# A gated relational graph layer on one core: smaller scans, two scales for the first weight, ScalarE in the closing of u, and a short path for tiles that only fill a turn

## The reference

```python
h = maximum(layernorm(x), 0)
u = h @ root + bias
for r in range(8):
    mask = edge_type == r
    sums = segment_sum(h[src] * mask[:, None], dst)     # [1250, 1024]
    cnt = segment_sum(mask, dst)
    u += (sums / maximum(cnt, 1)[:, None]) @ weight[r]
z = concatenate([u, h]) @ w_gate + b_gate
out = x + tanh(u) * z + h * (1 - z)
```

## Time and profile before

| | |
|---|---|
| median of 3 runs | 1389.53 us (1387.79 to 1394.82) |
| the profiled execution | 1388.87 us |
| its span, first to last instruction | 1387.1 us |
| granted TensorE clock, mean | 0.98 |
| busy: TensorE, VectorE, ScalarE, GpSimd | 1286.5, 962.9, 405.1, 791.4 us |
| moved by DMA | 269.42 MB, 194 GB/s |

### The profile page before, as it was taken

The page is one execution under the profiler, slowest core; times in us unless marked ns, Lnnn a source line. Parts: engine busy times, 40 slices in busy tenths (PEclk is TensorE's granted clock), DMA queues, the critical chain, the costliest instruction groups (busy, mean ns, idle before and its releaser), DMA issues.

```text
span 1387.1 us, 20131 instructions
## 1 busy us (share of the span) xinstructions
PE 1286.5 (93%) x6205; PEld 649.5 (47%) x6205; DVE 962.9 (69%) x1253; ACT 405.1 (29%) x496; POOL 791.4 (57%) x880
## 2 busy tenths in 40 slices
PE   2988889999999999999999999999899889988898
PEld 1434334444444445555554545444445444434565
DVE  5888678456564765677557767566575647998886
ACT  5344113224333430432232233222311211454100
POOL 2424078786878685777768766866675544431000
PEclk9999999999999999999999999999999999999999
DMA  6443115215214458776767888588786996677976
GB/s 224 155 172 107 44 38 173 63 45 174 54 45 116 131 171 272 238 224 193 246 211 231 270 276 284 162 296 272 230 259 218 349 304 182 207 250 220 250 228 188
DMA packets 112473, 269.42 MB, mean 194 GB/s; under 512 B 22678, under 2 KB 23181, under 8 KB 112388
## 3 DMA queue, kind: packets, MB, share of 16 engines
q1 hardware_dynamic: 75204, 175.63, 37.8%
q0 software_dynamic: 37184, 92.64, 23.6%
HBM read 203.66 MB, written 87.30 MB: 210 GB/s over the span
## 4 chain that ended last, share of the span: by engine, by line
PE 58%; DVE 14%; DMA 11%; issue 8%; POOL 4%; ACT 3%; POOLq 1%; DVEq 0%; SPq 0%; ACTq 0%
PE ps L1343 49%; DMA early<-y_rows,pair 9%; PE ps L1305 8%; DVE W L972 2%; POOL early L638 1%; DVE hT L1025 1%; POOL onehot L646 1%; DVE hT L1020 1%; POOL pair L628 1%; ACT W L752 1%; DMA early<-u_rows 1%; DVE yhl L1094 1%; ACT peek_out L719 1%; DVE urow L1185 1%; ACT early L762 1%
## 5 line engine op out<-in xcount | busy, mean ns | idle before, releaser
L1343 PE MATMUL ps<-W,hT 128*128 128x512 f16 (+2 forms) x4740 | 1073.5, 384 | 13.0 <-DVE W L972 13.0
L1343 PEld LDWEIGHTS ps<-W,hT 128*128 128x128 f16 (+2 forms) x4740 | 477.2, 103 | 532.9 <-issue 37.5
L638 POOL DMA_INDIRECT early<-y_rows,pair x200 | 240.4, 1202 | 132.1 <-PE ps L1308 81.6
L611 POOL DMA_INDIRECT table_rows<-edges,table_i x160 | 239.2, 1495 | 99.8 <-issue 99.8
L1305 PE MATMUL ps<-early,onehot 128*125 x800 | 206.8, 386 | 29.3 <-POOL onehot L646 15.5
L646 POOL TENSOR_SCALAR onehot<-iota_d,pair 128x125 f16<-128x125 f16 x188 | 160.8, 855 | 69.1 <-DMA early<-y_rows,pair 62.6
L972 DVE SCALAR_TENSOR_TENSOR W<-W,wsc 128x2048 f16<-128x2048 f32 x62 | 146.4, 2363 | 18.0 <-ACT W L752 18.0
L1305 PEld LDWEIGHTS ps<-early,onehot 128*125 x800 | 107.0, 137 | 103.9 <-issue 52.9
L752 ACT ACTIVATE W<-W,wsc 128x2048 f16<-128x2048 f32 x62 | 122.7, 1991 | 103.9 <-DVE W L988 51.3
L802 ACT ACTIVATE yhl<-early 128x512 f16<-128x512 f32 x100 | 62.8, 628 | 305.5 <-DVE early L1094 182.8
L719 ACT ACTIVATE peek_out<-W 128x1024 bf16<-128x1024 f32 x80 | 84.3, 1053 | 128.7 <-DMA W<-in_L_gnn_weight_dram 61.9
(11 more groups left out here) (187 smaller groups left out, 839.4 us busy)
## 6 DMA issues: line engine op xcount, KB each, us to landing
y_rows<-yhl SPq DMA_DIRECT2D x144, 256.0 KB, 2.7
W<-in_L_gnn_weight_dram SPq DMA_DIRECT2D x30, 1024.0 KB, 7.9
u_rows<-early SPq DMA_DIRECT2D x50, 448.0 KB
early<-u_rows SPq DMA_DIRECT2D x30, 448.0 KB
W<-in_L_gnn_w_gate_dram SPq DMA_DIRECT2D x8, 1024.0 KB, 7.1
early<-in_x_dram SPq DMA_DIRECT2D x9, 512.0 KB, 4.5
hs_rows<-early SPq DMA_DIRECT2D x9, 512.0 KB, 3.2
root_rows<-yhl SPq DMA_DIRECT2D x18, 256.0 KB, 5.5
```

What stands on the lines that cost most here:

```text
L611: pool.indirect_dma_start(out=table_rows, out_offset=bass.IndirectOffsetOnAxis(ap=at_i[:, c:c + 1], axis=0), in_=packed[0:EP, c:c + 1], in ...
L638: pool.indirect_dma_start(out=G[:, b, :], out_offset=None, in_=y_rows[i], in_offset=bass.IndirectOffsetOnAxis(ap=idx[:, b, :], axis=0), bo ...
L1343: last = nc.tensor.matmul(ps[0:rows, n % 4, :], hT[:, m, v_h, k, n0:n0 + rows], Wh[MAT[w][c]][:, v_w, k, :], start=(first and v_h + v_w == ...
```

## The change

- **Half scales.** Weight 0 gets one scale for its left half (quadrants 0, 1) and one for its right half (quadrants 2, 3). The lists ahead of unit 0 are written anew: one x tile and two quadrants first; `LEAD` goes from 2 to 3, with tile 1's transposes in the middle of unit 0, and the second scale's matmul behind unit 0. The first four units become (0,0), (1,0), (0,1), (1,1) in (row tile, half). SP issues x0, quadrants 0 and 1, x1, quadrants 2 and 3. `add_group` of relation 0 uses two reciprocals and two multiplies of 512 columns.
- **Small scans.** `scan_part` takes 16 parts of 5 groups (800 elements), spread over units 6 to 17; the keys come at unit 3; totals and bounds at units 18 and 20 (14 and 16 before). GpSimd fills the scan's factors behind row tiles 0 and 1. `positions` comes at units 22, 25, 28 and 32, after the low halves of weights in VectorE's list.
- **The sweeps** start at unit 113, not 100, and end where they did; the first three are packed closer.
- **Closing of u.** ScalarE sums the absolute values of the row (`u_size`) in place of VectorE's maximum, and ScalarE copies both banks out.
- **Fill tiles.** A sweep is rounded up so that at least one tile of its last turn is spare; TensorE's loop for the last group stops at the last tile with edges (`t_end`), and the spare tiles get only the count's matmul (`empty_tile`). GpSimd gathers and builds one-hots for them as before.

```diff
-    AGG_AT = ([100 + g * 63 // 30 for g in range(30)] + [164 + g * 42 // 20 for g in range(20)]
-              + [208 + g * 40 // 20 for g in range(20)] + [249 + g * 20 // 10 for g in range(10)])
+    AGG_AT = ([113 + g * 57 // 30 for g in range(30)] + [170 + g * 38 // 20 for g in range(20)]
+              + [209 + g * 39 // 20 for g in range(20)] + [249 + g * 21 // 10 for g in range(10)])
...
-    LEAD = 2
-    NORM_AT = {0: 2, 1: 3, 3: 4, 5: 5, 7: 6, 8: 7, 10: 8, 12: 9}
-    TURN_AT = {1: 2, 3: 3, 5: 4, 7: 5, 9: 6, 10: 7, 12: 8, 14: 9}
+    LEAD = 3
+    NORM_AT = {1: 3, 3: 4, 5: 5, 7: 6, 8: 7, 10: 8, 12: 9}
+    TURN_AT = {2: 2, 4: 3, 5: 4, 7: 5, 9: 6, 10: 7, 12: 8, 14: 9}
...
-    KEYS_AT, SCAN_AT, TOTALS_AT, BOUNDS_AT = 2, {4: 0, 7: 1, 10: 2, 12: 3}, 14, 16
-    POSITIONS_AT = {18: 0, 22: 1, 26: 2, 30: 3}
+    SN = 16
+    KEYS_AT, TOTALS_AT, BOUNDS_AT = 3, 18, 20
+    SCAN_AT = {6: (0, 1), 8: (2,), 9: (3,), 11: (4, 5), 12: (6,), 13: (7, 8), 14: (9,), 15: (10, 11), 16: (12, 13), 17: (14, 15)}
+    POSITIONS_AT = {22: 0, 25: 1, 28: 2, 32: 3}
...
             load_x(0)
+            for q in range(2):
+                land(0, q)
             load_x(1)
-            for q in range(4):
+            for q in range(2, 4):
                 land(0, q)
...
+            store_h(2)
+            load_x(4)
...
+            def u_size(j):
+                act.wait_ge(s["u_rooted"], j + 1)
+                if j:
+                    act.wait_ge(s["u_summed"], j)
+                nc.scalar.activation(u_abs[0:DT, :], cu[j % NCU][0:DT, :], ACT.Abs,
+                                     accum_out=urow[0:DT, j % 2:j % 2 + 1]).then_inc(s["u_summed"], 1)
...
-                act.wait_ge(s["uT_a"], j + 1)
                 act.wait_ge(s["gemm_done"], phase_end(W_GH, 1 if j < HT else 3))
-                nc.scalar.activation(hT[:, m, :, :, n0:n0 + DT],
...
+                for bank, turned, out_of in ((4, "uT_a", "uT_a_out"), (5, "uT_b", "uT_b_out")):
+                    act.wait_ge(s[turned], j + 1)
+                    nc.scalar.activation(hT[:, m + bank - 4, :, :, n0:n0 + DT],
...
-            for i in range(LEAD):
-                norm(i)
-            for i in range(LEAD):
-                turn_out(i)
+            norm(0)
             peek(0, 0)
-            peek(0, 1)
-            for c in range(4):
-                high_weights(0, c)
+            turn_out(0)
+            high_weights(0, 0)
+            high_weights(0, 1)
+            norm(1)
+            peek(0, 2)
+            turn_out(1)
+            high_weights(0, 2)
+            high_weights(0, 3)
+            norm(2)
...
-                step(nc.vector.tensor_scalar(turn_f[:, 0, 0:NS], ps[:, 7, NG:NG + NS], (RING - 1) / 2, 1.0 / RING, ALU.add, ALU.mult))
+                step(nc.vector.tensor_scalar(turn_f[:, 0, 0:NS], ps[:, 7, NG:NG + NS], (RING + 1) / 2, 1.0 / RING, ALU.add, ALU.mult))
...
             def row_scale(j):
-                u = cu[j % NCU][0:DT, :]
-                dve.wait_ge(s["u_rooted"], j + 1)
-                step(nc.vector.tensor_reduce(urow[0:DT, 0:1], u, AX.X, ALU.max, apply_absolute_value=True))
+                dve.wait_ge(s["u_summed"], j + 1)
...
+            stats_of(0)
+            first_peek(1)
+            dve.wait_ge(s["consts"], NCONST)
+            weight_top(0, 0)
+            weight_scale(0, 0)
+            turn_out(0)
+            stats_of(1)
+            low_weights(0, 0)
+            low_weights(0, 1)
             first_peek(3)
-            dve.wait_ge(s["consts"], NCONST)
-            weight_top(0)
-            weight_scale(0)
-            for c in range(4):
-                low_weights(0, c)
+            weight_top(0, 1)
+            turn_out(1)
+            weight_scale(0, 1)
+            stats_of(2)
+            low_weights(0, 2)
+            low_weights(0, 3)
...
+            def empty_tile(t):
+                pe.wait_ge(s["tile_ready"], t + 1 + RING)
+                hot_t = onehot[:, :, :].rearrange("p b n -> p (b n)")[:, bass.ds((t % RING) * P, DT)]
+                nc.tensor.matmul(ps[0:DT, 6, 0:2], hot_t, ones_h[:, :], start=False, stop=True,
+                                 skip_group_check=True).then_inc(s["onehot_free"], 1)
...
+                t_end = pe.value_load(bounds[0:1, NG + 1 + sweep:NG + 2 + sweep], min_val=2, max_val=TMAX)
+                with pe.Fori(t0 + 1, t_end) as t:
                     sum_tile(t, False)
+                with pe.Fori(t_end, t1) as t:
+                    empty_tile(t)
```

117 lines of the change are left out of this document (63 added, 54 removed).

## The result

The kernel after takes 1382.4 us (median of 10 executions, 1375.9 to 1383.8); the kernel before, with the executions added beside it, 1389.7 (10 executions, 1385.4 to 1394.8). The ratio is 0.9937, 95% interval 0.9917 to 0.9957: 6 to 12 us faster, where 41 were forecast. The forecast of 1348 and its range to 1370 both miss. Two of its own three alarms went off: the sweeps took over 630 us, and the closing still took 118 us or more.

The account below looks back on a forecast made before the run. The prediction took TensorE's product loop, busy 93% of the span, as the bound. Start 28, less 5 for new stops, plus 6.6 spare tiles and 12 closing gave 41.6 us off 1388.9: 1347.3, stated as 1348, range 1330 to 1370.

Parts of the forecast that it names:

- three alarms: Forecast wrong if unit 20 starts after 160, sweeps exceed 630 us, or closing's u transposes take 118 us or more.
- The start: Up to unit 20: first product at 22.2, unit 20 at 148.8 against 177.1, so 28 us sooner (16 to 33).
- 3.1 + 4 + 8: Losses charged before unit 20: 3.1 us stop before unit 2, 4 us slow matmuls, 8 us lost to VectorE.
- The aggregation's start: Positions at 160.5, GpSimd's scatters not moved; TensorE at unit 113 at 502.7, GpSimd at about 497, so 28 us stand.
- (c): Rival, units 4 to 19: VectorE bounds as before, 20 us lost, not 8; sums start 12 us later: 1360, chance 0.12.
- (d): Rival, slower: table late, each us of unit 22's finishes after 160.5 is lost; at 49 us late 1396, chance 0.03.
- (e): Rival, start: stays at 29.8 because quadrant 1 lands no sooner: 1355, chance 0.08.
- The sweeps: 13 units come out of the first three sweeps; 5 us of new stops charged (0 to 15).
- (a): Rival, sweeps: GpSimd's pace bounds them, they end where they did and only the closing gains: 1377, chance 0.10.
- Spare tiles: Sweep ends: 12 tiles that only fill up get the count's matmul alone, gaining 6.6 us (3 to 8.6).
- The closing: Closing of u: moving work from VectorE to ScalarE gains 12 us (3 to 19).
- (b): Rival, closing: gives 3 us, because VectorE then waits for ScalarE's size: 1357, chance 0.12.

Follow-up runs that it names:

- the repeated kernel: The kernel after, unedited, run again on another chip: 1379.1 us, ratio to before 0.9924.
- light feed: Every gather fetches only one row and one-hots are built in two columns: on the kernel after 1356.5 us, on the kernel before 1362.7 us.
- e1: The kernel after with the aggregation's groups back at the units of the kernel before, first at unit 100: 1386.5 us, ratio to before 0.9981.
- wide ends: The kernel after with four or five product units between sweeps, not two or three: 1376.9 us; with one-row gathers and two-column one-hots too, 1351.3 us.
- another lag: The kernel after with a tile's one-hot built after two more gathers instead of three, 1477.0 us, or after four, 1410.6 us.

## Why the prediction was wrong, point by point

**The start, right as a sum.** Forecast: unit 20 at 148.8; it starts at 149.7, 27.4 us sooner. Inside, two errors cancel. The first product is 4.2 us late on the forecast, and the rows show where. All engines in order of time, in the kernel after,

```profile
11.64 2.75 POOL L604 MEMSET hT<- 125x3180 bf16 x1
...
12.99 4.38 DVE L980 TENSOR_SCALAR wspread<-ones_f,wtop 128x128 f32<-128x128 f32 x1
...
14.38 2.79 POOL L604 MEMSET hT<- 125x3180 bf16 x1
17.10 0.19 POOL L605 MEMSET hT<- 125x20 bf16 x1
```

and in the kernel before:

```profile
22.71 0.28 DVE L950 TENSOR_SCALAR wspread<-ones_f,wtop 128x128 f32<-128x128 f32 x1
```

The peeks are done at 12.7 us, near the forecast's 12.4. Then the small step that spreads the maximum takes 4.38 us and not 0.28, and ends 0.08 us after GpSimd's fill of the scan's factors, which the change moved there from behind row tiles 2 and later. The same pair meets again at 31 us (5.09 us, to the end of the next fill), and in all eighteen profiles here with the new start the step takes 4.2 to 4.6 us, in the two with the old start 0.28 or 0.29. The prediction had put this move at nothing, as GpSimd "waits for tiles anyway"; it did not ask what VectorE does beside it. No run moves the fills alone, so the cause is read from these rows and not tested. From the scale to the first product it then takes 6.8 us, where 7.0 were forecast. The later losses are smaller: 123.3 us from first product to unit 20, less 111.5 of work, is 11.8, where 3.1 + 4 + 8 were charged. The granted clock is 1.00 there, 0.92 before.

**The aggregation's start, right.** The first scatter is at 176.3 (forecast 175.7), the first count at 504.1 (forecast 503.6). Rivals (c) and (d) fall with these two points, and (e) with the first product at 26.4. A small term hid a cancellation: the groups of VectorE that answer to the earlier trace rows, in the kernel after,

```profile
L1057 DVE TENSOR_TENSOR_SCAN hT<-hT 125x800 bf16<-125x800 bf16 x16 | 29.2, 1824 | 0.6
L1052 DVE TENSOR_TENSOR hT<-edges,iota_g 125x800 fp8e4<-125x800 f32 x16 | 17.6, 1103 | 0.0
```

take 46.8 us together, the four and four of before 46.7, so that the 24 more instructions seem to cost 0.1 us, where 4.8 were charged. But the mean of 8.18 us of a scan before is a mix:

```profile
L1025 DVE TENSOR_TENSOR_SCAN hT<-hT x4: 6824/8630/8632, 69.0 to 130.8; 125x3200 bf16<-125x3200 bf16 x4
```

(shortest, median and longest in ns). The 6.82 us scan has no work of GpSimd beside it; each of the three of 8.63 has GpSimd's low part of a row tile (L586) beside its start. Undisturbed, four small scans take 7.30 us for 6.82, and four small compares 3.92 (0.98 each in the middle of the sixteen) for 3.48: 0.15 to 0.16 us more for each added instruction, 3.7 us for 24. An estimate by the fixed latency of every instruction with an SBUF source (the Trainium skill, VectorE: DVE Perf Modes, The TRN2 errata — SBUF-src ops pay a fixed extra latency per instruction) is 3.8 us, and the trace agrees. What made it good again are the three stretched scans of before, 5.4 us, less 2.0 us of two compares that are stretched after (1.67 and 2.27 us).

**The sweeps, the step that failed.** "It is close. I charge 5 us of new stops (0 to 15)" was the term; it measured 17 to 24 us. The sweeps should have fallen by the 33.7 us of 13 units; they fell by 10.1 in this pair of profiles, so 24 came back as stops, and by 17.1 with the repeated kernel, so 17. (By the loss it is 32 and 25, 69.5 or 62.5 less 37.4, because the 8.6 us of the spare tiles are counted in it; they stand below as a term of their own.) The step compared means, 2.04 us for a tile on GpSimd against 2.8 to 3.1 that a tile would get, and took the idle 16.4 us of the second sweep as a reserve that can be spent. It isn't one. GpSimd waits because the ring is full, and TensorE waits at other times because it is empty (83.0 and 29.1 us in the same sweeps of the kernel after): tiles come in bursts of two or three, a new sweep needs three gathers before its first one-hot, and each gather needs some 6 us to land. The nearest rival, (a), had the place right and the reason too narrow: it held GpSimd's pace fixed, but with the light feed GpSimd waits 188 us for TensorE, and 31 us of extra loss are still there (up to 8.6 of them the spare tiles'). The gathers did not stretch more than before: they average 1191 ns, 1202 before, and 15 of 200 take over 1.5 us in either kernel. These 15 all have a long pass of VectorE beside them, while those with no VectorE instruction over 0.4 us beside them take 1.11 at most. That fits the port lock between VectorE and GpSimd (the Trainium skill, Trainium Architecture — The Big Picture, What this means for kernel authors), as the stretched steps of VectorE above do; that it would stretch gathers more as VectorE's work is packed closer is not borne out.

What is shown: 13 units fewer in the sweeps bring 15 to 22 us of loss at the same code (e1 beside the kernel after and its repeat), and neither light feed, nor wide ends, nor another lag returns it. What is only argued: that the rest at light feed, some 15 us inside the sweeps, is TensorE's own setting up of a group and its wait for VectorE's add, uncovered because the tiles come just in time. The waits named "issue" (5.7 us, 0.7 in the kernel before with the light feed, 11.6 with wide ends) and on L1215 (6.8, beside 4.5) point there; nothing here tests it. A rival is left for this part: with the light feed the new tile code itself may cost more than the 1 us of e1. The kernel with the old places and the light feed, which would tell, was not run.

**Spare tiles, mis-sized.** 6.6 us forecast, none measured. The prediction had named the reason (the last one-hots cost GpSimd 0.8 us each) and took only 2 of 8.6 us off for it. The rows at 729 to 731 us show it: the short matmuls come 0.7 us apart, at GpSimd's pace, and what TensorE saves it waits for at the next sweep's first one-hot.

**The closing, mis-sized.** 12 us forecast, 3.0 in the stage, none in the time. This is rival (b), at its price. VectorE did fall, from 109.3 to 94.3 us busy, and the 6.07 us stop on its copy is gone. Who VectorE waited for in that stage:

```profile
DVE uexp L1220 <- ACT edges L822: 11.4, 5, 3.3
DVE early L1228 <- ACT early L830: 6.4, 5, 3.2
DVE hT L1177 <- DMA hT<-zh_rows: 4.6, 1, 4.6
```

and TensorE:

```profile
PE ps L1378 <- ACT hT L844: 5.1, 3, 2.7
PE ps L1385 <- DVE hT L1188: 3.5, 2, 2.0
PE ps L1313 <- DVE wspread L980: 3.4, 1, 3.4
```

VectorE was spared 15 us of work, and waits 11.4 for ScalarE's size of u (L822), which it did not wait for before; on ScalarE's high part (L830) it waits 6.4, 3.7 before. The prediction took half of the stage's loss as the gain by VectorE's share, where the work was a chain from engine to engine, and moving a link of it does not shorten it.

In all: the 28 held; the 5 should have been 24 in this pair, the 6.6 nothing and the 12 should have been 3. 28 - 24 + 0 + 3 = 7 us, which is what was measured. That the 28 held is in part luck, as 4.1 us lost in the spreading step were made good by smaller losses behind it. Rivals (a) and (b) both held in their effect; together the prediction had them at 1386 and gave that 0.03, when they should have been weighed as likely: both ask only that waiting time on an engine is no slack.

## What to carry to other kernels

Independent matmuls that lie between dependent ones are cover, and pulling them out to another place saves only as much as the chain they covered does not need: before counting a stage shorter, add up what each piece of the feed takes at its worst (here three gathers and their landing at a sweep's start: 7.8 us from the last spare tile at 730.7 to the first tile at 738.5), not at its mean. An engine that waits in a full ring has no slack if its reader waits on the empty ring in the same stage. When a step is moved to a time in which its own engine is free, look at what the other engines do just then. And test a theory of a shared cost on the kernel before as well: the light feed on the new kernel alone seemed to prove one that the same feed on the old one refuted.

## What was not expected of the hardware

The lag is much sharper than its 6 us of landing suggests: one gather less ahead costs 95 us, 0.47 a tile, one more costs 28.

Short stops are dearer than they look, as the matmuls behind a stop run slower: after the 4.64 us stop the four matmuls of a tile take 1.96 us, and 1.03 to 1.07 elsewhere. It is the clock. The kernel after by stretch: the last products before the stop, the stop, the first tiles behind it, and two stretches more (columns as in the earlier trace rows):

```profile
731.00:734.00 3.00, 2.75 (x12) 1.10 (x12) 2.93 (x4) 0.00 (x0) 2.28 (x3) 1.00 0.21 22
734.00:738.40 4.40, 0.00 (x0) 0.00 (x0) 1.52 (x2) 0.63 (x1) 3.93 (x6) 0.81 0.60 183
738.48:742.50 4.02, 3.73 (x10) 2.04 (x11) 0.00 (x0) 0.00 (x0) 3.11 (x5) 0.50 0.77 248
742.50:746.00 3.50, 3.50 (x16) 1.67 (x15) 1.79 (x4) 0.00 (x0) 3.03 (x6) 0.85 0.37 86
746.00:750.00 4.00, 4.00 (x22) 2.10 (x20) 1.81 (x4) 2.52 (x2) 3.56 (x6) 1.00 0.87 263
```

The granted clock falls during the stop and is 0.50, the lower level of 1.2 GHz, for the tiles behind it; by 746 us it is full again. In the mean of the whole sweep this shows only as 0.98, where the kernel before with the light feed has 1.00.

And VectorE and GpSimd are not independent: a 0.28 us step of VectorE took 4.38 beside GpSimd's fill, a scan 8.63 for 6.82, and a gather up to 3.18 for 1.08.
